# Two-layer network, second layer: delta-rule queues reordered, expert stage entered by batches

## Chip, core and metric

The kernel runs on one core of one Trainium2 chip, in a single program. The metric is the device time of one execution in microseconds (us). Before the change the median of three runs is 2874.5 us (2872.1 to 2878.21).

## What is computed

The reference is a network of two layers on x of shape (8, 512, 128): 8 batches of 512 tokens, all in float32. Layer 0 (attention with 16 heads, then 8 experts with top-1 routing) isn't touched. Layer 1, cut to what matters:

```
h = layernorm(x) * (1 + ca) + sa
q, k, v = split(silu(causal_conv(h @ W_qkv)))      # 16 value heads of 64, 8 key heads
per token t:  S = S * exp(g_t);  S = S + k_t (v_t - k_t S) * b_t;  o_t = q_t S
x = x + ga * ((rmsnorm(o) * norm_w * silu(h @ W_z)) @ W_out)
h = layernorm(x) * (1 + cb) + sb
scores = sigmoid(h @ gate_w.T)                     # 16 experts
each expert takes its 512 best tokens: silu(g) * up, down, times score, added back
shared = (silu(h @ sh_gate.T) * (h @ sh_up.T)) @ sh_down.T
x = x + gb * (experts + shared)
```

## The kernel before

The program is a row of stages. Each stage has its own semaphores and ends in a barrier of all engines (Stage.end), and in a stage every engine works off its own queue in the order in which it is written. Three stretches matter here.

**The delta rule** (delta1, main loop on lines 1896 to 2497). The 8 batches of 512 tokens are worked as 4 pairs of sequences beside each other: one chunk step k (0 to 31) takes 32 tokens of four batches at once, with two halves f of eight heads. An even and an odd step make a pair m = k // 2. The loop variable k runs from FIRST to LAST, and the work is staged: in the iteration of k, the projections and the causal convolution for k + 4 are made (project, conv, squash), the norms, the decayed products and the triangular solve for the pair m + 1 (norms, diag, attend, turn, initial, substitute, turn_back), the recurrence itself for k (read_out, residual, solve, weights, attend on TensorE, weigh, add_state, update, decay), and the output for k - 1 (square_out, squares, total, root_out, inverse_norm, gated, turned, output).

- VectorE has the long piece: substitute (lines 2106 and 2107), 30 rounds of two instructions for a pair, spread over the two steps. In an even step it also has norms, two attends (a scan on line 2082, two products on 2089 and 2092, a copy on 2093) and turn (2097). update (2122) subtracts what add_state (2424) put into a bank from the state S.
- GpSimd has window (1916), diag (1923), residual (1929), decay (1941), weigh (1950), gated (1957, 1961), initial (1979 to 1984). In an even step diag stands ahead of residual; diag waits for norms on VectorE.
- ScalarE has square_out (2184), roots (2190), root_out (2196), project (2204 to 2215), weights (2251), values (2239), squash (2226), keys (2257), gate (2245), turned (2263), output (2270).
- TensorE has project (2335), read_out (2374), norms (2324), similar (2395), solve (2407), values (2351), attend (2438), add_state (2424), keys (2359), gate (2344), turned (2447) and output (2454). Small products share two banks of PSUM in turn; the list MISC fixes their order, and TensorE and ScalarE count through it.

**The entry of the expert stage.** residual1 loads the delta rule's output for all 4096 tokens (Hr) and four modulation rows (MODB), and adds ga * Hr to X (2515, 2516). A second stage loads the router's and the shared expert's weights and turns them on TensorE (1179 to 1184), with copies on VectorE (1192 to 1196). A third, norm_router, makes the statistics of all 32 tiles (819, 822), then batch by batch scales on VectorE (829), modulates (833, 834), turns (884), routes (892), and computes the shared expert: hidden (901, 903), silu (871), product (817), down (912), output (860).

**The selection** (same function, the stage that begins on line 1215). The threshold of each expert is found by 30 steps of bisection (BITS):

```
for n in range(BITS):                       # VectorE, lines 1313 to 1320
    count scores >= cand per partition      # 1315
    nxt = cand | next bit                   # 1317
    wait for the sum over partitions        # TensorE, 1372
    cand = nxt ^ (bit if sum < 512)         # 1319, 1320
```

In the first 24 of these steps TensorE also turns one third of an expert's weights (1379, 24 such units for experts 0 to 7), which ScalarE copies to SBUF (1258), while SyncE loads further experts' weights into two buffers (fetch, 1209, 1210). After the loop VectorE computes ranks and one-hot masks (1322 to 1345), and TensorE the lists of slots (1399).

## Time and profile before

| | us |
|---|---|
| median of 3 runs | 2874.5 |
| the profiled execution: its own time | 2889.17 |
| the profiled execution: span | 2887.4 |
| TensorE busy | 2208.4 (76%) |
| VectorE busy | 1884.6 (65%) |
| ScalarE busy | 1313.1 (45%) |
| GpSimd busy | 847.9 (29%) |

The profile is of one execution. An engine's busy time is the union of its instructions' durations; waits are what lies between. In the views, PE is TensorE's matmul, PEld its weight load, DVE VectorE, ACT ScalarE, POOL GpSimd, SPq the queue of SyncE that issues DMAs. L2107 is line 2107 of the kernel. In a timeline, a row gives start, duration, engine, line, instruction, what it writes and reads, how many were merged (x4), and in brackets how long the engine was idle before it and for whom it waited. PEclk is the clock that TensorE was granted, as a share of 2.4 GHz.

### The profile page before, as it was taken

The numbers are of one execution on the slowest core, as the hardware profiler recorded it, in microseconds if no ns is written. First come the engines' busy times: TensorE is split into PE (matmuls) and PEld (weight loads), VectorE is DVE, ScalarE is ACT, GpSimd is POOL, SyncE is SP. The second block draws the span as 40 slices with busy tenths as digits, with TensorE's granted clock in tenths as the row PEclk, the third lists the DMA queues.
The fourth block names the chain that finished last, engine by engine and source line by source line (L and its number), as shares of the span: only waits on it lengthen the run. The fifth ranks groups of instructions, "written<-read, shape, count | busy, mean of one in ns | idle before, by whom it ended". The sixth has DMA issues, their size and how long they took to land. (4 is left out here: it accounts for less than half of the span.)

```text
span 2887.4 us, 63254 instructions
## 1 busy us (share of the span) xinstructions
PE 2208.4 (76%) x25656; PEld 1394.9 (48%) x25656; DVE 1884.6 (65%) x4425; ACT 1313.1 (45%) x2383; POOL 847.9 (29%) x877
## 2 busy tenths in 40 slices
PE   2798889888888573488888888888888862755984
PEld 0344444444444361355555555565555541544653
DVE  1477667767666226588888888888888834254433
ACT  0367667666655221555555555555555230121321
POOL 1000010100100240135555445444554530002885
PEclk8599889989978796579988888898988885757997
DMA  5000000000000412100000000000000002142334
GB/s 198 7 1 5 5 8 5 8 5 5 9 4 5 118 53 61 26 9 11 11 12 12 11 11 12 11 12 12 11 11 4 4 10 89 42 117 69 54 44 84
DMA packets 104290, 85.49 MB, mean 30 GB/s; under 512 B 22126, under 2 KB 90898, under 8 KB 103616
## 3 DMA queue, kind: packets, MB, share of 16 engines
q1 hardware_dynamic: 90432, 68.31, 8.0%
q0 software_dynamic: 13568, 13.14, 2.8%
q8 instruction: 203, 3.33, 0.5%
q14 instruction: 87, 0.71, 0.1%
HBM read 59.22 MB, written 22.71 MB: 28 GB/s over the span
## 5 line engine op out<-in xcount | busy, mean ns | idle before, releaser
L617 ACT ACTIVATE Pr<-Pr,nmax 128x512 f32<-128x512 f32 x512 | 341.2, 714 | 181.3 <-DVE nmax L552 179.0
L722 PE MATMUL bank<-ident,Pr 128*128 128x128 f32 x2048 | 322.6, 303 | 71.6 <-DVE PT L561 59.0
L722 PEld LDWEIGHTS bank<-ident,Pr 128*128 128x128 f32 x2048 | 249.2, 154 | 260.7 <-DVE PT L561 152.8
L552 DVE CUSTOM_DVE_ANT_0 Pr<-bank,Tb 128x512 f32<-128x512 f32 x512 | 331.1, 685 | 46.9 <-PE bank L708 46.9
L561 DVE COPY PT<-bank 128x512 f32<-128x512 f32 x256 | 176.5, 689 | 194.1 <-PE bank L736 189.1
L2351 PE MATMUL bank<-Wcv,hw 128*128 128x512 f32 x512 | 276.4, 690 | 7.5 <-POOL hw L1916 4.5
L2107 DVE TENSOR_TENSOR Tc<-Tc,pr 128x30 f32<-128x30 f32 (+14 forms) x480 | 209.1, 436 | 16.5
L624 ACT ACTIVATE PT<-bank 128x512 f32<-128x512 f32 x256 | 151.0, 590 | 121.4 <-PE bank L736 86.0
L2106 DVE TENSOR_TENSOR pr<-AC,Tc 128x30 f32<-128x30 f32 (+14 forms) x480 | 190.7, 397 | 17.5 <-POOL Tc L1984 3.7
L708 PE MATMUL bank<-kp,qp 8*128 8x512 f32 x1024 | 181.0, 707 | 1.1 <-DVE nmax L552 1.1
L2351 PEld LDWEIGHTS bank<-Wcv,hw 128*128 128x128 f32 x512 | 107.5, 221 | 131.5 <-issue 118.9
L2215 ACT ACTIVATE yp<-raw,cwq 128x256 f32<-128x256 f32 x384 | 160.1, 508 | 0.0
L736 PE MATMUL bank<-PT,vp 128*9 128x512 f32 x1024 | 156.1, 683 | 0.0
L432 POOL DMA_INDIRECT disp<-H,slot x32 | 31.8, 993 | 399.2 <-DVE slot L508 391.9
L2407 PE MATMUL bank<-Xs,Tt 32*32 32x64 f32 x4096 | 87.0, 243 | 67.4 <-POOL Xs L1929 67.4
L1929 POOL TENSOR_TENSOR Xs<-vt,Xs 128x512 f32<-128x512 f32 x64 | 94.6, 1488 | 149.2 <-DVE Xs L2019 149.2
L423 POOL TENSOR_SCALAR H<-X,rs,nm 128x128 f32<-128x128 f32 x32 | 14.0, 452 | 423.0 <-DVE nm L540 423.0
L2407 PEld LDWEIGHTS bank<-Xs,Tt 32*32 32x32 f32 x4096 | 76.8, 141 | 90.2 <-issue 68.1
L1941 POOL TENSOR_TENSOR S<-S,GC 128x1024 f32<-128x1024 f32 x60 | 114.6, 1909 | 0.0
L1438 POOL DMA_INDIRECT acc<-eo,ids x64 | 100.8, 1576 | 39.4 <-issue 18.6
L2374 PE MATMUL bank<-S,kq 64*32 64x128 f32 x4096 | 108.7, 275 | 2.4 <-DVE S L2122 2.4
L2122 DVE TENSOR_TENSOR S<-S,bank 128x512 f32<-128x512 f32 x120 | 76.9, 682 | 51.4 <-PE bank L2424 51.4
(397 smaller groups left out, 4419.1 us busy)
## 6 DMA issues: line engine op xcount, KB each, us to landing
aB<-alpha SPq DMA_DIRECT2D x64, 128.0 KB, 2.8
Tb<-scores SPq DMA_DIRECT2D x1, 7168.0 KB
w<-in_L_ffn_W SPq DMA_DIRECT2D x16, 256.0 KB, 5.8
rawW<-in_L_ffn_up_w SPq DMA_DIRECT2D x16, 256.0 KB, 3.0
rawW<-in_L_ffn_gw SPq DMA_DIRECT2D x16, 256.0 KB, 3.4
rawW<-in_L_ffn_down_w SPq DMA_DIRECT2D x16, 256.0 KB, 3.8
disp<-zero SPq DMA_DIRECT2D x1, 2580.0 KB, 15.6
xin<-disp SPq DMA_DIRECT2D x8, 322.5 KB, 6.4
```

The source lines that it names most:

```text
L552: V.tensor_tensor_reduce(out=Pr[:, s, i, :], in0=pS[hh][:, :], in1=Tb[:, h, at:at + L], scale=-1.0, scalar=3.0e38, op0=ALU.add, op1=ALU.mi ...
L561: V.tensor_copy(PT[:, m % NPS, :], pT[m % 2][:, :]).then_inc(r["b_evd"], 1)
L617: A_(Pr[:, s, i, :], Pr[:, s, i, :], ACT.Exp, scale=-1.0, bias=nmax[:, s, i:i + 1])\
L624: A_(PT[:, m % NPS, :], pT[m % 2][:, :], ACT.Copy).then_inc(r["b_eva"], 1)
L708: mm(pS[hh][:, :], qp[rows, G % SLOTS, i * P:(i + 1) * P], kp[rows, G % SLOTS, :], start=True, stop=True, tile_position=(32 * hh, 0)).then ...
L722: last = TR(pT[m % 2][:, t * P:(t + 1) * P], Pr[:, (G % 2) * HG + hh, t, j * P:(j + 1) * P], ident[:, :])
L736: mm(pO[32 * hh:32 * hh + HD0 + 1, :], vp[:, b % 2, j, G % NG * HG + hh, :], PT[:, m % NPS, :], start=(j == 0), stop=(j == LT - 1), tile_p ...
L2106: link(V.tensor_tensor(o, bcast(AC[:, i + 1:CK, i], 2, i), bcast(Tc[:, i, 0:i], 1, n), ALU.mult))
L2107: link(V.tensor_tensor(Tc[:, i + 1:CK, 0:i], Tc[:, i + 1:CK, 0:i], o, ALU.add))
L2215: last = A_(yp[:, i, j, :, :], raw[:, tp, j, :, i:i + 2 * CK], ACT.Copy, scale=tap(j, i))
L2351: last = mm(o[:, :], tokens(k, i), Wcv[:, i, 512 * f:512 * f + 512], start=(i == 0), stop=(i == KS - 1))
L2407: last = mm(BK[f][rows, DK * h:DK * h + DK], Tt[rows, :, k % 2, HF * f + h], Xs[rows, f, DK * h:DK * h + DK], start=True, stop=True, tile_ ...
```

## The change

Four things change.

1. Delta rule, output: the product with W_out for step k - 1 isn't issued at the end of the iteration of k any more, but in the next one, on TensorE behind the first projection and ahead of read_out, on ScalarE behind the first project. MISC has it in the new place, and the DMA out follows.
2. Delta rule, orders. GpSimd: both residuals ahead of diag, and initial ahead of the second decay. VectorE: both read_outs first, conv ahead of the second squares, the second conv between the two attends, inverse_norm behind turn (in an odd step behind the second conv), and rounds 18 to 30 of the substitution cut at 20 and 25. ScalarE: the second square_out behind project and output, weights(k, 0) ahead of the second project, root_out behind it.
3. Entry: the three stages become one (entry1), which goes batch by batch: load of Hr and of three rows, residual, statistics, root, scaling on GpSimd, modulation, turn, route. The shared expert is taken out of it; hT keeps the turned tokens of all 8 batches.
4. Selection: the shared expert is put between the counting steps. In steps 4b and 4b + 1 TensorE computes hidden(b, 0) and hidden(b, 1), in steps 4b + 2 and 4b + 3 the halves of down(b - 1), and every second step (12 in place of 24) turns a unit of weights; the other 12 units come behind the loop. VectorE has product in steps 4b + 1 and 4b + 2, ScalarE the silu and the copy out, SyncE the writes to acc between the loads of the experts 2 to 7.

The delta rule:

```diff
 
-            FIRST, LAST = -4, NS + 1
+            FIRST, LAST = -4, NS + 2
             MISC = []
             for k in range(FIRST, LAST):
                 if (k + 4) // 2 < NP:
                     MISC += [("pj", 2 * (k + 4))]
+                if 0 <= k - 2 < NS:
+                    MISC += [("out", k - 2)]
                 if k % 2 == 0 and 0 <= k // 2 + 1 < NP:
                     MISC += [("nm", k // 2 + 1)]
@@ -1864,7 +1935,7 @@
                 if 0 <= k < NS:
                     MISC += [("z", 2 * k), ("z", 2 * k + 1)]
                 if 0 <= k - 1 < NS:
-                    MISC += [("ot", 2 * (k - 1)), ("ot", 2 * (k - 1) + 1), ("out", k - 1)]
+                    MISC += [("ot", 2 * (k - 1)), ("ot", 2 * (k - 1) + 1)]
             USE = {key: u for u, key in enumerate(MISC)}
...
                         m, e = k // 2, k % 2
                         if 0 <= k + 1 < NS:
                             window(k + 1)
+                        if 0 <= k < NS:
+                            residual(k, 0)
+                            residual(k, 1)
                         if 0 <= m + 1 < NP and e == 0:
                             diag(2 * (m + 1))
                         if 0 <= k < NS:
-                            residual(k, 0)
-                            residual(k, 1)
                             decay(k, 0)
                         if 0 <= m + 1 < NP and e == 0:
                             diag(2 * (m + 1) + 1)
                         if 0 <= k < NS:
                             weigh(k, 0)
                             weigh(k, 1)
-                            decay(k, 1)
                         if 0 <= m + 1 < NP and e == 0:
                             initial(m + 1)
+                        if 0 <= k < NS:
+                            decay(k, 1)
                         if 0 <= k - 1 < NS:
...
                             squares(k - 1, 0)
                         if here:
                             read_out(k, 0)
+                            read_out(k, 1)
+                        if (k + 4) // 2 < NP:
+                            conv(2 * (k + 4))
                         if past:
                             squares(k - 1, 1)
                             total(k - 1)
-                        if here:
-                            read_out(k, 1)
-                        if (k + 4) // 2 < NP:
-                            conv(2 * (k + 4))
                         if ahead and e == 0:
                             norms(m + 1)
-                        if 0 <= k - 1 < NS:
-                            inverse_norm(k - 1)
-                        if ahead and e == 0:
                             attend(2 * (m + 1))
-                            attend(2 * (m + 1) + 1)
-                            turn(m + 1)
                         if ahead and e == 1:
                             substitute(m + 1, 12, 18)
                         if (k + 4) // 2 < NP:
                             conv(2 * (k + 4) + 1)
+                        if ahead and e == 0:
+                            attend(2 * (m + 1) + 1)
+                            turn(m + 1)
+                        if past:
+                            inverse_norm(k - 1)
+                        if ahead and e == 1:
+                            substitute(m + 1, 18, 20)
                         if here:
                             accumulate(k, 0)
                             update(k, 0)
                         if ahead and e == 0:
                             substitute(m + 1, 1, 6)
                         if ahead and e == 1:
-                            substitute(m + 1, 18, 24)
+                            substitute(m + 1, 20, 25)
                         if here:
                             accumulate(k, 1)
                             update(k, 1)
                         if ahead and e == 0:
                             substitute(m + 1, 6, 12)
                         if ahead and e == 1:
-                            substitute(m + 1, 24, CK - 1)
+                            substitute(m + 1, 25, CK - 1)
                             turn_back(m + 1)
 
                 @block.scalar
                 def _(act):
                     A_ = nc.scalar.activation
 
...
                         if past:
-                            square_out(k - 1)
+                            square_out(k - 1, 0)
                         if (k + 4) // 2 < NP:
                             project(2 * (k + 4))
+                        if 0 <= k - 2 < NS:
+                            output(k - 2)
+                        if past:
+                            square_out(k - 1, 1)
                         if k % 2 == 0 and 0 <= k // 2 + 1 < NP:
                             roots(k // 2 + 1)
+                        if here:
+                            weights(k, 0)
+                        if (k + 4) // 2 < NP:
+                            project(2 * (k + 4) + 1)
                         if past:
                             root_out(k - 1)
-                        if (k + 4) // 2 < NP:
-                            project(2 * (k + 4) + 1)
-                        if here:
-                            weights(k, 0)
                         if 0 <= k + 1 < NS:
                             values(k + 1, 0)
                         if here:
                         if past:
                             turned(k - 1, 0)
                             turned(k - 1, 1)
-                            output(k - 1)
...
                         if (k + 4) // 2 < NP:
                             project(2 * (k + 4))
+                        if 0 <= k - 2 < NS:
+                            output(k - 2)
                         if here:
                             read_out(k, 0)
                             read_out(k, 1)
...
                         if past:
                             turned(k - 1, 0)
                             turned(k - 1, 1)
-                            output(k - 1)
```

The entry (lines that only moved are left out):

```diff
+def entry1(nc, g, a, s, w, hT):
...
+        def _(sp):
+            def batch(b):
+                sp.dma_start(of(Hr, b), g["attn"][b * L:(b + 1) * L, :].rearrange("(t p) d -> p t d", p=P))\
+                  .then_inc(s[f"n_in{b}"], 16)
+                sp.dma_start(rows[:, b, :, :], bcast(g["mods"][1, b, GA:CB + 1, :], 0, P)).then_inc(s[f"n_in{b}"], 16)
+            batch(0)
...
+                sp.dma_start(d, v).then_inc(s["n_ld"], 16)
+            for b in range(1, B):
+                batch(b)
+            sp.dma_start(w["gbr"][:, :, :, :], mod_rows(g, 1, GB, GB + 1)).then_inc(s["n_db"], 16)
+            sp.dma_start(w["dbias"][:, :, :], bcast(a["L1_ffn_down_b"], 0, P)).then_inc(s["n_db"], 16)
...
+            def residual(b):
+                dve.wait_ge(s[f"n_in{b}"], 32)
+                link(V.tensor_tensor(of(Hr, b), of(Hr, b), row(b, GA), ALU.mult))
+                V.tensor_tensor(of(X, b), of(X, b), of(Hr, b), ALU.add).then_inc(s["n_x"], 1)
...
+            def inverse(b):
+                at = slice(b * LT, (b + 1) * LT)
+                dve.wait_ge(s["n_rstd"], b + 1)
+                link(V.reciprocal(rs[:, at], rs[:, at]))
+                V.scalar_tensor_tensor(nm[:, at], mv[:, at, 0], -1.0, rs[:, at], ALU.mult, ALU.mult)\
+                    .then_inc(s["n_nm"], 1)
+
+            def modulate(b):
+                dve.wait_ge(s["n_hs"], b + 1)
+                link(V.tensor_tensor(of(H, b), of(H, b), row(b, CB), ALU.mult))
+                V.tensor_tensor(of(H, b), of(H, b), row(b, SB), ALU.add).then_inc(s["n_h"], 1)
...
+            residual(0)
+            stats(0)
+            dve.wait_ge(s["n_t"], 1)
...
             for b in range(B):
+                if b + 1 < B:
+                    residual(b + 1)
+                inverse(b)
+                if b + 1 < B:
+                    stats(b + 1)
                 if b:
                     logits(b - 1)
-                    if shared:
-                        product(b - 1)
+                modulate(b)
...
+        @block.gpsimd
+        def _(pool):
+            for b in range(B):
+                pool.wait_ge(s["n_nm"], b + 1)
+                for n in range(b * LT, (b + 1) * LT):
+                    last = nc.gpsimd.tensor_scalar(H[:, n, :], X[:, n, :], rs[:, n:n + 1], nm[:, n:n + 1],
+                                                   ALU.mult, ALU.add)
+                last.then_inc(s["n_hs"], 1)
...
+            root(0)
             for b in range(B):
                 if b + 1 < B:
-                    turned(b + 1)
+                    root(b + 1)
+                act.wait_ge(s["n_xT"], b + 1)
+                A_(hT[:, b, :], PB[b % 2][:, :], ACT.Copy).then_inc(s["n_hT"], 1)
...
+            pe.wait_ge(s["n_e"], 1)
             for b in range(B):
-                if b + 1 < B:
-                    turn(b + 1)
+                turn(b)
                 route(b)
```

The selection, on VectorE and on TensorE (ScalarE follows TensorE's order):

```diff
+                    def product(b, c):
+                        dve.wait_ge(s["h_up"], 2 * b + c + 1)
+                        dve.wait_ge(s["h_sg"], 2 * b + c + 1)
+                        if b >= 2:
+                            dve.wait_ge(s["h_so"], b - 1)
+                        V.tensor_tensor(su[:, b % 2, c, :], PB[3 + c][:, :], sg[:, c, :], ALU.mult).then_inc(s["h_su"], 1)
...
                     for n in range(BITS):
                         bit = BITS - 1 - n
                         V.tensor_scalar(junk[:, :], sT[:, :], cand[:, :].bitcast(F32), None, ALU.is_ge, ALU.add,
                                         accum_out=acc[:, :]).then_inc(s["h_acc"], 1)
                         link(V.tensor_scalar(nxt[:, :], cand[:, :], (1 << bit) >> 1, None, ALU.bitwise_or))
+                        if n % 4 in (1, 2):
+                            product(n // 4, n % 4 - 1)
                         dve.wait_ge(s["h_cnt"], n + 1)
                         link(V.tensor_scalar(off[:, :], PB[1][:, 0:1], float(CAP1), float(1 << bit), ALU.is_lt, ALU.mult))
...
                     V.tensor_tensor_scan(cum[:, :], one[:, :], eq[:, :], 0.0, ALU.mult, ALU.add).then_inc(s["h_gt"], 1)
+                    product(B - 1, 1)
                     dve.wait_ge(s["h_nd"], 1)
...
+                    def prepare(m):
+                        e, kind = m // 3, m % 3
+                        pe.wait_ge(s[f"h_ld{e % 2}"], 48 * (e // 2 + 1))
+                        if m >= 3:
+                            pe.wait_ge(s["h_wte"], m - 2)
...
+                    def hidden(b, c):
+                        if b or c:
+                            pe.wait_ge(s["h_sg"], 2 * b + c)
+                        mm(PB[2][:, :], wg[:, c * P:(c + 1) * P], hT[:, b, :], start=True, stop=True)\
+                            .then_inc(s["h_gp"], 1)
+                        if b:
+                            pe.wait_ge(s["h_su"], 2 * (b - 1) + c + 1)
+                        mm(PB[3 + c][:, :], wu[:, c * P:(c + 1) * P], hT[:, b, :], start=True, stop=True)\
+                            .then_inc(s["h_up"], 1)
+
+                    def down(b, t0):
+                        pe.wait_ge(s["h_su"], 2 * b + 2)
+                        if b:
+                            pe.wait_ge(s["h_soe"], b)
+                        for t in (t0, t0 + 1):
+                            for c in range(2):
+                                last = mm(PB[0][:, t * D:(t + 1) * D], su[:, b % 2, c, t * P:(t + 1) * P],
+                                          wd[:, c, :], start=(c == 0), stop=(c == 1))
+                        if t0:
+                            last.then_inc(s["h_so"], 1)
                     pe.wait_ge(s["h_mk"], 1)
                     for n in range(BITS):
                         pe.wait_ge(s["h_acc"], n + 1)
                         mm(PB[1][:, 0:1], blk[:, :], acc[:, :], start=True, stop=True).then_inc(s["h_cnt"], 1)
-                        if n < 3 * EA:
-                            e, kind = n // 3, n % 3
-                            pe.wait_ge(s[f"h_ld{e % 2}"], 48 * (e // 2 + 1))
-                            if n >= 3:
-                                pe.wait_ge(s["h_wte"], n - 2)
-                            for c in range(FC):
-                                last = TR(PB[5 + kind][:, c * P:(c + 1) * P], raw[:, e % 2, kind, c, :], ident[:, :])
-                            last.then_inc(s["h_wt"], 1)
+                        b, u = n // 4, n % 4
+                        if u < 2:
+                            hidden(b, u)
+                        elif b:
+                            down(b - 1, 2 * (u - 2))
+                        if early(n) is not None:
+                            prepare(early(n))
+                    prepare(LATE)
...
+                    down(B - 2, 0)
+                    down(B - 2, 2)
                     pe.wait_ge(s["h_sel"], 1)
                     mm(PB[1][:, 2:3], low[:, :], cum[:, L - 1:L], start=True, stop=True).then_inc(s["h_pre"], 1)
+                    prepare(LATE + 2)
+                    prepare(LATE + 3)
+                    down(B - 1, 0)
+                    down(B - 1, 2)
                     pe.wait_ge(s["h_pos"], 1)
```

gbr holds the rows for the last residual; the old stages and residual1 are removed.

## Rows read from the trace of the kernel before

**Rows 1.** Windows of the run: span, busy time of each engine, granted clock, DMA.

```profile
core 0: us, PE busy (x) PEld busy (x) DVE busy (x) ACT busy (x) POOL busy (x), PEclk, DMA share, GB/s
...
1218.80:2269.20 1050.40, 884.77 (x16777) 616.13 (x16775) 903.81 (x1752) 559.67 (x1154) 507.18 (x529) 0.88 0.04 11
...
2380.20:2417.40 37.20, 2.54 (x9) 1.54 (x9) 10.23 (x8) 0.00 (x0) 0.00 (x0) 0.50 0.47 154
2417.40:2529.40 112.00, 74.54 (x288) 53.01 (x288) 41.24 (x138) 19.86 (x34) 0.00 (x0) 0.75 0.13 38
...
2533.20:2580.60 47.40, 37.59 (x146) 27.91 (x146) 28.44 (x126) 14.33 (x24) 0.00 (x0) 0.50 0.50 140
```

**Rows 2.** The tile AC: count, min/median/max ns, first and last start.

```profile
L2097 DVE STREAM_TRANSPOSE AC<-A x16: 1245/1245/1247, 1218.8 to 2269.2; 128x1024 f32<-128x1024 f32 x16
L1979 POOL TENSOR_TENSOR AC<-AC,rkT x16: 1909/1913/1918, 1220.2 to 2272.1; 128x1024 f32<-128x1024 f32 x16
L1981 POOL TENSOR_SCALAR_AFFINE_SELECT Tc<-AC x16: 1266/1267/1267, 1222.1 to 2274.1; 128x1024 f32<-128x1024 f32 x16
```

**Rows 3.** Waits of VectorE from 1218.8 to 2269.2 us (total, times, longest).

```profile
DVE S L2122 <- PE bank L2424: 43.6, 27, 3.6
DVE bank L2070 <- ACT yp L2215: 25.9, 27, 1.0
DVE Lt L2082 <- POOL Lt L1923: 18.4, 16, 1.2
DVE A L2089 <- PE bank L2395: 13.5, 15, 2.1
DVE pr L2106 <- POOL Tc L1984: 3.5, 11, 1.5
```

**Rows 4.** Timeline of TensorE, an odd step (1716.5 to 1749.3 us).

```profile
1727.45 1.09 PE L2438 MATMUL bank<-Ws,Pt 32*32 32x64 f32 x64 [2.12 <-ACT Ws L2251]
1728.48 5.40 PE L2351 MATMUL bank<-Wcv,hw 128*128 128x512 f32 x8
```

**Rows 5.** Timeline of TensorE in the router stage: hidden, down, hidden.

```profile
2434.40 2.05 PE L901 MATMUL bank<-hT,wg 128*128 128x512 f32 x2
...
2517.36 2.05 PE L912 MATMUL bank<-wd,su 128*128 128x128 f32 x16
2519.24 1.02 PE L901 MATMUL bank<-hT,wg 128*128 128x512 f32 x2
```

**Rows 6.** Timeline of GpSimd and TensorE, the even step behind rows 4.

```profile
1757.30 1.05 POOL L1923 TENSOR_TENSOR Lt<-bk,d 128x512 f32<-128x512 f32 x1 [15.82 <-DVE rkd L2061]
...
1759.72 1.94 PE L2407 MATMUL bank<-Xs,Tt 32*32 32x64 f32 x64 [4.19 <-POOL Xs L1929]
```

**Rows 7.** Timeline of the entry on VectorE: residual, statistics, modulation.

```profile
2394.76 4.42 DVE L2515 TENSOR_TENSOR Hr<-Hr,MODB 128x4096 f32<-128x4096 f32 x1 [29.38 <-DMA Hr<-attn]
...
2417.38 6.29 DVE L819 BATCH_NORM_STATS2 st<-X 128x6 f32<-128x128 f32 x32 [0.93 <-PEq L86]
...
2427.97 0.69 DVE L833 TENSOR_TENSOR H<-H,MODB 128x512 f32<-128x512 f32 x1
```

**Rows 8.** Timeline of VectorE: the substitution's smallest shape, behind initial and at the end.

```profile
1703.72 0.98 DVE L2106 TENSOR_TENSOR pr<-AC,Tc 128x30 f32<-128x30 f32 x1 [0.19 <-POOL Tc L1984]
...
1747.70 0.19 DVE L2106 TENSOR_TENSOR pr<-AC,Tc 128x30 f32<-128x30 f32 x1
```

**Rows 9.** The scaling of the tile H on GpSimd in layer 0 (L423).

```profile
L423 POOL TENSOR_SCALAR H<-X,rs,nm x32: 445/452/454, 260.0 to 959.1; 128x128 f32<-128x128 f32 x32
```

**Rows 10.** Timeline of TensorE in the bisection: a count and a unit of turning.

```profile
2535.96 0.58 PE L1372 MATMUL bank<-hits,blk 128*128 128x1 f32 x2 [0.35 <-DVE junk L1315]
2536.41 1.09 PE L1379 MATMUL bank<-ident,rawW 128*128 128x128 f32 x4
```

**Rows 11.** Groups of VectorE, 1218.8 to 2269.2 us: the substitution.

```profile
L2107 DVE TENSOR_TENSOR Tc<-Tc,pr 128x30 f32<-128x30 f32 (+14 forms) x450 | 193.4, 430 | 15.5
L2106 DVE TENSOR_TENSOR pr<-AC,Tc 128x30 f32<-128x30 f32 (+14 forms) x450 | 176.6, 392 | 16.4 <-POOL Tc L1984 3.5
```

331 lines of the change are left out of this document (143 added, 188 removed).

## The prediction

> **What bounds the kernel now.** I cut the run into windows first, at the places where the code changes stage, since a busy share over the whole run mixes stages with different limits. The change touches four of them [rows 1]: the steady part of the delta rule, 1050.4 us; the residual and the loads ahead of the router, 37.2; the router with the shared expert, 112.0; and the bisection, 47.4 for 25 of its 30 steps. Look at three things in these rows. In the delta rule VectorE is busy 903.8 of 1050.4 us (86%) and TensorE 884.8 (84%): either may bound it, and both wait. In the 37.2 us almost nothing computes. In the router stage TensorE is busy 74.5 of 112 us at a mean clock of 0.75, VectorE 41.2: nothing is full, the engines take turns. In the bisection the clock is 0.50 throughout, though TensorE is busy for 37.6 of 47.4 us.
>
> The delta rule's period comes from a tile written once for each pair of steps: 16 times from 1218.8 to 2269.2 us, so 1050.4 / 15 = 70.0 us a pair [rows 2]. The waits of VectorE in this window sum to 106.6 us with a sixth one of 1.7 [rows 3], that is 7.1 us a pair. VectorE's queue is nearly gapless otherwise, so a pair can't get shorter than about 70.0 - 7.1 = 62.9 us however the other engines are ordered.
>
> **Delta rule, wait by wait.** The instructions stay the same, so what counts is which of these waits goes and what is late next.
> - *S on add_state, 43.6 us.* In odd steps attend on TensorE waited 2.12 us for Ws, since weights stands behind ScalarE's second project, and the eight matmul instructions after it took 5.40 us [rows 4]; two of this width take 2.05 us at half clock and 1.02 at full clock [rows 5], so that this was partly a half-clock stretch behind an idle one. In even steps solve waited 4.19 us for the residual on GpSimd, which stood behind diag, and diag had waited 15.82 us for VectorE's norms [rows 6]. Residual ahead of diag and weights ahead of the second project remove both. What is late next: in even steps TensorE meets the second similar, which may only overwrite its bank when the first attend on VectorE is through, some 2 us after TensorE gets there. Kept: 1 us a pair, 15 us.
> - *The bank on yp, 25.9.* The first conv waits for project, which stood behind two square_outs, the second of them held by VectorE's squares. Now only one stands ahead. Kept: 0. The second project now waits for solve in its place, through weights; conv for it comes behind the whole first attend, which covers that.
> - *The scan on Lt, 18.4.* The second attend waited; three conv instructions now stand between. But the first diag (1.05 us) [rows 6] runs between norms and the first scan, and inverse_norm, which filled that, is moved behind turn. Kept: 0.75 a pair, 11 us.
> - *A on similar, 13.5.* Same cover. Kept: 0.
> - *The substitution on Tc, 3.5.* Behind turn GpSimd has initial, 1.91 + 1.27 us and a small memset [rows 2]. Conv, accumulate and update covered that; now it is inverse_norm, accumulate and update only, about 2.4 us. This wait grows to 0.8 a pair, 12 us.
>
> Kept in all 15 + 11 + 12 = 38 us, gained 106.6 - 38 = 68 us, or 4.5 a pair. Bounds: 107 if none is left; at the other end nothing, or less (rivals). Output a place later: TensorE runs the first project while ScalarE copies OT, so it no longer stalls ahead of output; that is in the sum already, as read_out comes earlier. The DMA out has a whole step to land, and SyncE's gates pass it only in order: nothing. The extra iteration holds one output that ended the loop before too: nothing.
>
> **Entry.** Before: 37.2 + 112.0 = 149.2 us [rows 1]. After: the first batch's Hr and rows are loaded first, then weights, turns and copies. The weight stage took 13.8 us: from 2394.76 + 2 x 4.42 = 2403.6 to 2417.4 [rows 1, 7]. Its largest load (1 MB) now comes last, batch 0 comes first instead; I keep 13.8, and residual(0) and stats(0) lie inside it. Then eight rounds on VectorE. One round: residual 2 x 0.69 [rows 7]; inverse, two tiny ones, 0.4 (the 30-element op alone takes 0.19 [rows 8]); then the scaling on GpSimd, 4 x 0.452 = 1.81 [rows 9], beside which VectorE makes the next statistics (6.29 / 8 = 0.79 and less for the aggregates [rows 7]) and the logits; then modulation 2 x 0.69. With 0.3 for hand-overs: 1.38 + 0.4 + 1.81 + 1.38 + 0.3 = 5.3, times 8 = 42. TensorE's turn and route of the batch before lie beside it. The tail is turn (four transposes, like a unit of the bisection), a copy, route (half the products of a down, 2.05 at most), the last write and the barrier (0.93 us of idling ahead of the statistics): I estimate 6. Sum 13.8 + 42 + 6 = 62. The loads (some 5.7 MB against 4 MB in the 14.6 us before the first instruction there) run ahead of rounds of 5.3 us. Gain 149 - 62 = 87 us; between 78 (rounds of 6.4) and 94.
>
> **Bisection.** The old step is 47.4 / 25 = 1.9 us. TensorE had 1.09 us of turning in it and still 0.35 us idle before the next count [rows 10], so about 1.45 us a step are free. At full clock hidden needs four such instructions, 2 x 1.02 less their overlap, 1.7 us, half a down 2.05 / 2 = 1.0 [rows 5], a unit of turning 0.55. Over four steps the excess is 0.3, 0.8 (hidden and unit), 0, 0.1: 1.2, times 7.5 = 9 us. VectorE's product (0.69) lies where VectorE waits for the count: 2 us in all. Behind the loop 1. At half clock hidden is 3.5, half a down 1.9, a unit 1.09: excess 2.0, 3.1, 0.5, 1.6 = 7.2, times 7.5 = 54 us, 57 with the rest. So it is 12 at one end, 57 at the other. The nearest row is the router stage's clock of 0.75, with idle stretches that the new loop lacks; the bisection's 0.50 is of turning and counting alone [rows 1]. I take 16. The last 8 units of turning lie beside the 48 instructions in which VectorE makes the masks: nothing.
>
> **Sum.** -68 - 87 + 16 = -139 us, on the profiled execution's 2889.17: 2750. It stands 0.5% above the median of 2874.5, and I carry the difference over: 2735 as a median.
>
> **Rivals.**
> 1. *The bisection stays at half clock.* For: 0.50 over 47 us at 79% busy. Against: that work was turning, and in the router stage the same products reached full clock, 1.02 for 2.05 [rows 5]. Then -68 - 87 + 57 = -98: 2776. Chance 0.14.
> 2. *The delta rule gains little.* The second similar waits, TensorE's clock halves behind it, and values and add_state come later by as much as the removed idle time gave. For: rows 4 show such a stretch behind 2.12 us. Then I give it 20 us instead of 68: -91: 2783. Chance 0.17.
> 3. *VectorE becomes the floor.* No wait is left, rounds of the entry are 4.5 us: -107 - 93 + 10 = -190: 2685. Chance 0.13.
> 4. *Slower: VectorE is held up by GpSimd in more places.* The substitution takes (193.4 + 176.6) / 15 = 24.7 us a pair [rows 11]; its smallest shape takes 0.19 us in one place and 0.98 where GpSimd's gated runs [rows 8]. Its place now: decay(k, 1) and gated both come behind initial, on top of substitute(1, 6). By what these rows show one meeting costs 0.8 us. For the whole kernel to be slower by over 0.2% it must cost (139 + 6) / 16 = 9 us a pair, eleven more meetings in each; at 10 us a pair the time would be 2735 + 160 = 2895. For: GpSimd has 529 / 15 = 35 instructions a pair [rows 1], so there are enough of them. Against: their number stays, and the old order has such meetings too. Up to 4.5 us a pair it only eats the delta rule's gain. Chance 0.03.
>
> The Trainium skill, page "SBUF — State Buffer", section "SBUF: two separate sides", has the rule for rival 4: a VectorE instruction with two inputs in SBUF and a GpSimd instruction that reads SBUF exclude each other for the whole instruction, with no sharing. The trace agrees (0.98 us against 0.19 for one shape), and by that rule an order alone can make VectorE's instructions longer or shorter.
>
> That the change doesn't do what it says, I give nothing: each move is written out in the queues.
>
> **Numbers.** The forecast has 0.53. Its own range is 2700 to 2765 (entry +-9, delta +-25, bisection -6 to +20). With the rivals: 2675 to 2790. About 0.2%, 6 us, is what a measurement can tell from no change. Faster: 0.53 + 0.14 + 0.17 + 0.13 = 0.97, less 0.01 that falls within 0.2%: 0.96; slower 0.03.
>
> **What the profile after would show.** The tile AC at intervals of 65.5 us; VectorE's wait on add_state below 20 us, on yp near 0, on Tc up to about 12; solve and attend no longer waiting over 2 us. From the end of the delta rule to the bisection 62 us. Count to count 1.9 to 2.5 us, with a clock near 1 there. I am wrong on the delta rule if the interval stays above 68 us, or if the substitution's sum grows by more than 3 us a pair; on the entry if the GpSimd scaling takes over 2.5 us a batch; on the bisection if the clock stays at 0.50.

## The result and the profile after

The changed kernel takes 2805.03 us (median of 4 runs, 2798.69 to 2808.58), the kernel before 2876.36 us in 4 runs beside it: a ratio of 0.9743 with a 95% interval of 0.9708 to 0.9778. It is faster, by 71 us, about half of the 139 us forecast, and outside the range of 2675 to 2790.

The windows of the run after, cut at the same stage boundaries, the columns those of [rows 1]:

```profile
0.00:1142.00 1142.00, 867.46 (x5183) 469.57 (x5184) 691.37 (x2012) 586.08 (x944) 114.10 (x155) 0.86 0.10 32
...
1197.50:2271.80 1074.30, 914.75 (x16775) 646.04 (x16774) 939.89 (x1745) 554.64 (x1151) 489.03 (x529) 0.85 0.04 11
...
2379.90:2440.80 60.90, 27.64 (x109) 22.20 (x109) 37.41 (x137) 8.96 (x20) 15.03 (x37) 0.50 0.47 140
2440.80:2501.80 61.00, 55.43 (x267) 36.39 (x268) 43.03 (x166) 20.41 (x34) 0.00 (x0) 0.95 0.36 97
```

and the tile AC, which answers to [rows 2]:

```profile
L2170 DVE STREAM_TRANSPOSE AC<-A x16: 1245/1245/1246, 1197.5 to 2271.8; 128x1024 f32<-128x1024 f32 x16
```

The profiled execution took 2798.69 us, 90.5 less than the one of before. By stage:

| stage | before, us | after, us | difference |
|---|---|---|---|
| up to the first AC (layer 0 and the delta rule's start) | 1218.8 | 1197.5 | -21.3 |
| AC to AC, 15 intervals | 1050.4 | 1074.3 | +23.9 |
| last AC to the entry | 111.0 | 108.1 | -2.9 |
| entry, from the end of the delta rule to the first count | 153.0 | 60.9 | -92.1 |
| bisection, 30 steps | 57.2 | 61.0 | +3.8 |
| the rest of the span | 297.0 | 294.9 | -2.1 |

Three things are to be read here. The entry did what was said of it. The bisection cost a quarter of what was said, at a granted clock of 0.95. And the delta rule, which was to gain 68 us, lost 24: the interval is 1074.3 / 15 = 71.6 us, where 70.0 was and 65.5 was forecast. The first line is not the change's: in e1_entry_only below, whose code up to there is that of before, the first AC comes at 1198.6 us, and in the other runs anywhere from 1188.4 to 1213.7.

Where VectorE and TensorE wait in that window (total, times, longest), to be held against [rows 3]:

```profile
DVE bank L2143 <- ACT yp L2288: 39.8, 13, 3.2
DVE rkq L2125 <- ACT rkq L2263: 21.1, 13, 4.0
DVE Lt L2155 <- POOL Lt L1994: 15.8, 16, 1.2
DVE S L2195 <- PE bank L2500: 5.5, 5, 3.1
...
PE bank L2500 <- DVE S L2195: 82.7, 27, 5.8
```

The waits on S (43.6 us, now 5.5) and A (now 0.2) are gone, as forecast. But yp, which was to wait for nothing, takes 39.8 us, rkq, for which it had waited 1.7 us in all, 21.1, and all of them, four small ones included, come to 93.1 us. The last line is the mirror image: TensorE, which waited 12.8 us for VectorE's state update before, now waits 82.7 for it. VectorE's busy time also rose, from 903.8 [rows 1] to 939.9 us. Its groups with the largest change (busy us, mean ns), in the window of after:

```profile
L2179 DVE TENSOR_TENSOR pr<-AC,Tc 128x30 f32<-128x30 f32 (+14 forms) x450 | 201.3, 447 | 16.0 <-POOL Tc L2055 3.6
L2180 DVE TENSOR_TENSOR Tc<-Tc,pr 128x30 f32<-128x30 f32 (+14 forms) x450 | 192.9, 429 | 15.5
...
L2119 DVE TENSOR_TENSOR nrm<-nrm,rkq 128x16 f32<-128x16 f32 x27 | 37.6, 1392 | 0.9
...
L2112 DVE TENSOR_TENSOR rq<-rkq 128x8 f32<-128x8 f32 x28 | 15.2, 542 | 1.0
...
L2166 DVE COPY dl<-Lt 128x16 f32<-128x16 f32 x30 | 6.4, 214 | 0.0
```

The same instructions took 370 us (the first two, [rows 11]), 13.8, 4.7 and 24.1 us before, at means of 492, 166 and 777 ns for the last three.

### The profile page after: what moved, and what is told of

The parts are those of the page before. It is cut to its first block and busy times, and to the rows that moved or that the text cites. A ratio compares the mean times of both kernels' runs of the same rounds, so it can differ in the third digit from the quotient of the medians.

```text
span 2796.7 us, 63261 instructions
## 1 busy us (share of the span) xinstructions
PE 2193.0 (78%) x25656; PEld 1397.8 (50%) x25656; DVE 1922.3 (69%) x4429; ACT 1308.5 (47%) x2389; POOL 842.6 (30%) x909
## 5 line engine op out<-in xcount | busy, mean ns | idle before, releaser
L722 PEld LDWEIGHTS bank<-ident,Pr 128*128 128x128 f32 x2048 | 238.5, 149 | 254.4 <-DVE PT L561 154.0
L722 PE MATMUL bank<-ident,Pr 128*128 128x128 f32 x2048 | 310.9, 294 | 69.5 <-DVE PT L561 59.2
L2427 PE MATMUL bank<-Wcv,hw 128*128 128x512 f32 x512 | 263.3, 661 | 8.5 <-POOL hw L1987 5.2
L2179 DVE TENSOR_TENSOR pr<-AC,Tc 128x30 f32<-128x30 f32 (+14 forms) x480 | 215.9, 450 | 16.9 <-POOL Tc L2055 3.6
L2500 PE MATMUL bank<-Ud,Kt 32*64 32x128 f32 x1920 | 79.4, 311 | 93.4 <-DVE S L2195 87.7
L736 PE MATMUL bank<-PT,vp 128*9 128x512 f32 x1024 | 150.4, 659 | 0.0
L2000 POOL TENSOR_TENSOR Xs<-vt,Xs 128x512 f32<-128x512 f32 x64 | 80.8, 1275 | 209.1 <-DVE Xs L2092 209.1
L423 POOL TENSOR_SCALAR H<-X,rs,nm 128x128 f32<-128x128 f32 x32 | 13.9, 448 | 404.9 <-DVE nm L540 404.9
L2500 PEld LDWEIGHTS bank<-Ud,Kt 32*64 32x64 f32 x1920 | 63.4, 153 | 120.9 <-issue 105.3
L2411 PE MATMUL bank<-hTa,Wqk 128*128 128x256 f32 x256 | 97.3, 519 | 17.9 <-ACT bank L2282 8.9
L2021 POOL TENSOR_TENSOR Ud<-Ws,dl 128x512 f32<-128x512 f32 x60 | 63.4, 1056 | 147.8 <-ACT Ws L2324 147.8
```

Of the source, the lines that this page charges most:

```text
L722: last = TR(pT[m % 2][:, t * P:(t + 1) * P], Pr[:, (G % 2) * HG + hh, t, j * P:(j + 1) * P], ident[:, :])
L736: mm(pO[32 * hh:32 * hh + HD0 + 1, :], vp[:, b % 2, j, G % NG * HG + hh, :], PT[:, m % NPS, :], start=(j == 0), stop=(j == LT - 1), tile_p ...
L2179: link(V.tensor_tensor(o, bcast(AC[:, i + 1:CK, i], 2, i), bcast(Tc[:, i, 0:i], 1, n), ALU.mult))
L2427: last = mm(o[:, :], tokens(k, i), Wcv[:, i, 512 * f:512 * f + 512], start=(i == 0), stop=(i == KS - 1))
L2500: last = mm(BK[x % 2][64 * r:64 * r + 64, P * q:P * q + P], Kt[rows, k % 2, P * q + 64 * r:P * q + 64 * r + 64], Ud[rows, r, P * q:P * q + ...
```

## The experiments

Each run was made beside the kernel before on the same chip, and the ratios are to that. "Interval" is AC to AC, first to last over 15, in one profiled execution of each kernel. It came out as 70.03 and 70.01 us in the two kernels that have the delta rule of before, and as 71.62 and 71.61 in the two that have the changed one, so I read differences of 0.3 us and more from it. The last column is the time for which add_state on TensorE waited for the state update S; waits of read_out for S aren't in it (15.0 us in f3, 18.1 in i1, 16.4 in i2, at most 5.9 in the others).

| run | median, us | ratio, 95% interval | interval, us | VectorE busy, us | TensorE on S, us |
|---|---|---|---|---|---|
| before | 2876.36 | | 70.03 | 903.8 | 12.8 |
| after | 2805.03 | 0.9743 [0.9708, 0.9778] | 71.62 | 939.9 | 82.7 |
| e1_entry_only | 2786.29 | 0.9685 [0.9641, 0.9729] | 70.01 | 904.4 | 12.8 |
| e2_delta_only | 2899.29 | 1.0096 [1.0066, 1.0126] | 71.61 | 940.2 | 84.7 |
| e3_weights_back | 2798.3, one run | | 70.71 | 930.9 | 62.2 |
| e4_inverse_back | 2821.1, one run | | 72.31 | 931.3 | 79.4 |
| f1_pool_only | 2773.55 | 0.9655 [0.9615, 0.9695] | 68.79 | 914.6 | 15.0 |
| f2_vector_only | 2838.84 | 0.9891 [0.9837, 0.9944] | 73.70 | 933.8 | 39.9 |
| f3_output_only | 2818.25 | 0.9821 [0.978, 0.9862] | 72.37 | 915.6 | 12.8 |
| f4_scalar_only | 2947.12 | 1.025 [1.0211, 1.0289] | 80.55 | 918.0 | 131.9 |
| g1_output_in_place | 2811.6 | 0.9781 [0.9737, 0.9824] | 72.53 | 945.9 | 83.4 |
| g2_pool_back | 2806.1 | 0.9765 [0.9719, 0.981] | 71.20 | 932.0 | 84.8 |
| g3_cut_20_25 | 2840.26 | 0.9895 [0.9853, 0.9937] | 73.95 | 938.8 | 71.5 |
| g4_cut_and_rows_ahead | 2796.92 | 0.9728 [0.9678, 0.9779] | 70.95 | 927.1 | 13.1 |
| h1_cut_back | 2739.14 | 0.9536 [0.9506, 0.9566] | 67.31 | 936.8 | 28.5 |
| h2_vector_no_cut | 2794.32 | 0.9742 [0.9704, 0.978] | 71.23 | 917.1 | 14.8 |
| h3_one_row | 2802.47 | 0.9761 [0.9729, 0.9793] | 71.55 | 923.7 | 42.0 |
| h4_residual_only | 2759.38 | 0.9593 [0.9558, 0.9629] | 68.51 | 913.2 | 24.5 |
| i1_inverse_sooner | 2731.46 | 0.951 [0.9459, 0.956] | 66.97 | 905.8 | 17.6 |
| i2_and_initial_back | 2730.93 | 0.9525 [0.9472, 0.9579] | 66.39 | 907.3 | 17.7 |

### The change in two halves

e1_entry_only is the changed kernel with the function delta1 of before; e2_delta_only is the kernel before with delta1 of after.

> The delta rule's function is that of before; entry and selection are the changed ones. Theory: the whole gain lies in entry and selection (94 us less in the entry, 4 us more in the bisection) and the delta rule's reordering gave back some 24 us. Then this kernel takes 2876 - 88 = 2788 us, less than the changed kernel's 2805, and the tile AC comes at intervals of 70.0 us. Rival (the traces' difference in the delta rule is a matter of the execution, not of the orders): the interval is 71.6 here as well and the time that of the changed kernel, 2805.

> The kernel before with the changed kernel's delta rule alone. Theory: AC at intervals of 71.6 us, 15 to 16 of them, so 2876 + 20 = 2896 us, 0.7% slower than before. Rival: no difference (interval 70.0, 2876 us).

The entry and the bisection alone beat the whole change, 0.9685 against 0.9743 (the 95% intervals of the two overlap by a little, their runs, up to 2791.14 us and from 2798.69 us on, don't), and the delta rule alone is slower than nothing, 1.0096. Both came as expected. Each has the interval and the waits of the kernel whose delta1 it has, so the two halves don't touch one another.

### Two moves undone

e3_weights_back puts weights back behind the second project on ScalarE; e4_inverse_back puts inverse_norm back behind norms on VectorE, with ScalarE's root_out where that needs it.

```
 ScalarE, e3:                      VectorE, e4:
-  weights(k, 0)                    norms(m + 1)
+  root_out(k - 1)                 +inverse_norm(k - 1)
   project(2 * (k + 4) + 1)         attend(2 * (m + 1))
-  root_out(k - 1)                  ...
+  weights(k, 0)                   -inverse_norm(k - 1)
```

> The changed kernel, on ScalarE alone root_out and the second project stand ahead of weights(k, 0) again. Theory: VectorE's second conv waited 39.8 us for yp because project stood behind weights, and weights behind solve; with the old order this wait is below 5 us, the wait on add_state returns only in odd steps, by under 20 us; the interval of AC falls by 1 to 2 us to about 70. Rival (VectorE's lengthened instructions are the whole cause): the wait moves but the interval stays within 0.5 us of 71.6.

> The changed kernel; inverse_norm stands behind norms again, ahead of the first attend, and on ScalarE root_out ahead of weights and of the second project, so that inverse_norm needn't wait for them. Theory: the product nrm by rkq, 1.39 us on average now because GpSimd's initial runs at the same time, falls to 0.5 us or less, 24 us in the stretch; the first scan's wait for GpSimd (15.8 us) falls below 8; the interval falls by 1.5 to 2.5 us. Rival: the length moves to other instructions (accumulate, substitution, the copy dl, 0.78 before and 0.21 now) and the interval stays within 0.5 us of 71.6.

With weights back yp's wait is 0, but a wait of 24.1 us on A and one of 19.3 on S stand in its place, and the interval falls by 0.9 us only. With the inverse back its own group falls to 13.7 us as expected, but the substitution grows to 414.9 us and S costs 31.7: the interval rises where a fall was expected. Both missed on the interval: the name on the longest wait was not its cause, since taking it away only renamed it.

### The four orders, one at a time

On e1_entry_only, each run takes one queue's hunk of the change's diff: GpSimd's (f1), VectorE's (f2), the output product a place later on all engines (f3), ScalarE's (f4). f1 and the core of f3:

```
 GpSimd, f1:                          f3 (MISC; ScalarE, TensorE, SyncE alike):
+  residual(k, 0), residual(k, 1)        MISC += [("pj", 2 * (k + 4))]
   diag(2 * (m + 1))                  +  if 0 <= k - 2 < NS:
-  residual(k, 0), residual(k, 1)     +      MISC += [("out", k - 2)]
   ...                                   ...
-  decay(k, 1)                        -  ..., ("out", k - 1)]
   initial(m + 1)
+  decay(k, 1)
```

> The new entry and bisection with the delta rule of before, whose one change is GpSimd's order: both residuals ahead of diag, initial ahead of decay(k, 1). In the rest of the delta rule all is as before. Without it the interval from AC to AC is 70.0 us and the time about 2786 us. Theory A (the loss of the changed kernel is VectorE's own order, by which it comes to yp and rkq before they are there): the interval stays within 0.4 us of 70.0 and the time at 2780 to 2792. Theory B (the loss is in the collisions with GpSimd, whose longest work now falls on VectorE's long rows): the interval grows by 0.8 us or more, the time to 2800 or more, and nrm<-nrm,rkq L2119 or the substitution takes longer than in before (492 ns and 370 us in all).

> The new entry and bisection with the delta rule of before, whose one change is VectorE's order: both read_outs and the first conv ahead of the second squares, one attend, the second conv, the other attend, inverse_norm late, the substitution cut at 20 and 25. Theory A: the loss is here: interval 71.0 or more, time 2800 or more, with waits on yp and rkq of 20 us and more each, since VectorE asks for them sooner and ScalarE still gives them late. Theory B (collisions that come from GpSimd's order): within 0.4 us of 70.0. Theory C (ScalarE's order makes yp late): the yp wait is under 10 us and the interval under 70.5.

> The new entry and bisection with the delta rule of before, whose one change is that the output product and all that belongs to it (PE, ScalarE's copy, SyncE's DMA) come a place later, behind the next first project. Theories A, B and C all say that this part does no harm by itself: TensorE doesn't wait for VectorE's turned output as long, and add_state's 12.8 us of waits on PE fall or stay. Interval 69.3 to 70.2, time 2775 to 2790. If it is instead this part that costs (the copy of the output now stands ahead of the second square and roots on ScalarE, 0.5 us or so a place), the interval is 71 or more.

> The new entry and bisection with the delta rule of before, whose one change is ScalarE's order: the first project ahead of the second square, weights(k, 0) ahead of the second project, root_out behind it; the output stays in its place. Theory C (the loss is that weights wait for PE's solve and hold up the second project): interval 71 or more with a wait on yp of 20 us or more. Theory A: VectorE takes the second conv late here, behind both attends, so yp is there: wait on yp under 5 us, and A's or S's wait falls since weights come earlier; but root_out now stands behind the second project, and inverse_norm is early in VectorE's order of before, so a wait on it shows up, some 10 to 20 us in all; interval 69.5 to 70.7.

GpSimd's order is a gain by itself (-1.2 us an interval), the first clear one; theory B falls. VectorE's costs 3.7, with yp at 42.9 us, so theory A stood for the moment. The output product costs 2.4 by itself. None of the three theories said so; the expectation named such a cost only as the other case, and put it down to ScalarE's copy. The rows point elsewhere: output took a turn between the first project and the norms, and the two banks for such products are given out in turn, so that the norms (L2396) and the second project (L2407) now need the bank that the first project just filled, and wait for ScalarE to copy it. Waits of TensorE in f3_output_only:

```profile
PE bank L2396 <- ACT bank L2280: 54.8, 13, 4.5
PE bank L2407 <- ACT bank L2280: 41.0, 13, 3.5
```

ScalarE's order alone costs 10.5 us an interval, far from either theory. Its root_out comes late while VectorE's inverse_norm is still early, 28 waits of 6.7 us. Waits of VectorE in f4_scalar_only:

```profile
DVE nrm L2114 <- ACT nrm L2264: 187.9, 28, 8.9
```

The single effects sum to +15.4 us, the four together to +1.6: two orders that are made for each other can't be priced apart.

### Taking parts out of the whole, and one small piece alone

g1 and g2 are the changed kernel with the output in its old place, and with GpSimd's old order. g3 and g4 go from f1 (GpSimd's new order, the best so far) and add one small piece of VectorE's order, the cut of the substitution: rows 18 and 19 ahead of the state update in the odd places.

```
 VectorE, g3 against f1:                 g4 besides:
-  substitute(m + 1, 12, 18)             +  substitute(m + 1, 12, 14)
+  substitute(m + 1, 12, 20)                conv(2 * (k + 4))
   conv(2 * (k + 4) + 1)                    ...
   accumulate(k, 0)                      -  substitute(m + 1, 12, 20)
   update(k, 0)                          +  substitute(m + 1, 14, 20)
-  substitute(m + 1, 18, 24)                conv(2 * (k + 4) + 1)
+  substitute(m + 1, 20, 25)
   ...
-  substitute(m + 1, 24, CK - 1)
+  substitute(m + 1, 25, CK - 1)
```

(conv stands behind the rows in both, as in the kernel before.)

> The changed kernel whose output product, its copy and its DMA stay at the end of their own place (the other three orders are the changed ones). Theory D, from the output product alone (72.37 us in place of 70.01): with the output between the first project and the norms, TensorE's norms need the bank that the first project has just filled, and wait until ScalarE has copied it, so rkq comes late. Without it the wait of VectorE on rkq falls from 21.1 us to under 5, and the interval of the changed kernel, 71.62, falls by 1 to 2 us, to 69.6 to 70.6; time 2775 to 2792. The rival: in the changed orders the norms are late for another reason (the project itself is asked for late), and the output's place has no effect: rkq still 15 to 25 us, interval 71.3 to 71.9, time about 2805.

> The changed kernel with GpSimd's order of before (diag ahead of the residuals, decay(k, 1) ahead of initial). GpSimd's order alone, on the old orders, gave 1.2 us an interval. If its gain is its own (the copy of dl no longer meets GpSimd, 24.0 to 5.5 us, and A's wait falls from 15.5 to 3.7), the interval of the changed kernel grows from 71.62 to 72.4 to 73.2, time 2817 to 2830. The rival: its gain hangs on the other orders, and with the changed ones its collisions (nrm<-nrm,rkq 37.6, rq 15.2 us) are its price: then the interval stays at 71.3 to 71.9 or falls, and L2119 and L2112 fall back to 14 and 5 us.

> The new entry and bisection, GpSimd's new order, and of the rest of the delta rule's change only the cut of the substitution: rows 18 and 19 ahead of accumulate and update in the odd places, not behind (12 to 20, 20 to 25, 25 to 31). In the kernel with GpSimd's order alone VectorE waits 2.3 us for add_state in every odd place, right behind accumulate; the two rows take 1.75 us. If they fill that wait, S's 25.3 us of waits fall by 15 or more and the interval from 68.79 to 67.3 to 68.1, time 2752 to 2766. The rival: the wait is only moved, since the second update and the products behind it start 1.75 us later in TensorE's and ScalarE's orders, or the two rows meet GpSimd: interval 68.6 to 69.2, time 2770 to 2780.

> As the cut at 20 and 25 on GpSimd's new order, and with rows 12 and 13 of the substitution ahead of the first conv in the odd places, where VectorE waits 0.95 us for yp. If the row work fills that wait too, yp's 22.0 us fall to about 10 and the interval lies 0.6 to 1.0 under that of the cut alone, 66.5 to 67.5, time 2740 to 2758. The rival: conv comes 0.8 us later, so squash, and the squares behind it on ScalarE, come later and the wait turns up at rkq or at the next yp: interval no lower than with the cut alone.

None came out as its theory said. Without the late output the changed kernel is slower, 72.53 for 71.62, though it costs 2.4 alone: with the other orders new it gains 0.9. Without GpSimd's order it is no slower (71.20), as g2's rival had it, but the two groups that were to fall back to 14 and 5 us (L2119 and L2112 above) are at 29.7 and 15.3. And the two rows that should have filled a wait of 2.3 us cost 5.2 us an interval. g4 has the same cut, and beside it two other rows taken from behind the first conv of the odd place to ahead of it: its interval is 70.95 us, 3.0 less than g3's, and add_state's wait for S falls from 71.5 us to 13.1. So rows ahead of the update don't all cost alike. With six rows between the first conv and the update again, as in f1, most of the loss is gone; which of g4's two differences from f1 makes the 2.2 us that remain, no run shows. The cut is the largest effect of so small a piece, and it is in the changed kernel too. The changed kernel's odd place, on VectorE from the second conv to the second update:

```profile
1721.54 1.22 DVE L2119 TENSOR_TENSOR nrm<-nrm,rkq 128x16 f32<-128x16 f32 x1
1722.68 0.39 DVE L2179 TENSOR_TENSOR pr<-AC,Tc 128x234 f32<-128x234 f32 x1
1723.11 1.13 DVE L2180 TENSOR_TENSOR Tc<-Tc,pr 128x234 f32<-128x234 f32 x1
1724.27 1.36 DVE L2179 TENSOR_TENSOR pr<-AC,Tc 128x228 f32<-128x228 f32 x1
1725.66 1.12 DVE L2180 TENSOR_TENSOR Tc<-Tc,pr 128x228 f32<-128x228 f32 x1
1726.82 0.69 DVE L2201 TENSOR_TENSOR O<-O,bank 128x512 f32<-128x512 f32 x1
1727.42 1.28 DVE L2195 TENSOR_TENSOR S<-S,bank 128x512 f32<-128x512 f32 x2
```

on GpSimd:

```profile
1720.83 1.90 POOL L2012 TENSOR_TENSOR S<-S,GC 128x1024 f32<-128x1024 f32 x1
1722.84 1.13 POOL L2028 TENSOR_TENSOR O<-O,nrm 128x512 f32<-128x512 f32 x1
1724.12 1.26 POOL L2032 TENSOR_TENSOR O<-O,zs 128x512 f32<-128x512 f32 x1
1725.34 1.19 POOL L2028 TENSOR_TENSOR O<-O,nrm 128x512 f32<-128x512 f32 x1
1726.67 1.27 POOL L2032 TENSOR_TENSOR O<-O,zs 128x512 f32<-128x512 f32 x1
```

and on TensorE:

```profile
1722.68 1.09 PE L2514 MATMUL bank<-Ws,Pt 32*32 32x64 f32 x64
1728.85 1.98 PE L2500 MATMUL bank<-Ud,Kt 32*64 32x128 f32 x32 [5.07 <-DVE S L2195]
1730.76 1.11 PE L2435 MATMUL bank<-ident,kq 128*128 128x128 f32 x4
...
1742.00 5.02 PE L2400 MATMUL bank<-bd,sqc 128*128 128x2 f32 x32
```

A row takes 0.4 + 0.4 us undisturbed. Beside GpSimd's gated output three of the four instructions end some 0.25 us after one of GpSimd's and take 1.1 to 1.4 us: 4.1 us from 1722.68 to the accumulate, where 1.75 was expected. Behind them stands the update, behind that TensorE's second add_state, which idles 5.07 us. Behind the idle time TensorE runs slower as well: this add_state takes 1.98 us, where the first one of the same place (1721.64) took 1.10, and the norms take 5.02, where they take 4.44 in h1 below. Over the window an instruction of add_state takes 312 ns on average, 273 before and 278 in h1, and the granted clock of the window, 0.88 before, is 0.85.

### The cut

h1 is the changed kernel with the old cut, everything else new:

```
-                        if ahead and e == 1:
-                            substitute(m + 1, 18, 20)
                         if here:
                             accumulate(k, 0)
                             update(k, 0)
...
-                            substitute(m + 1, 20, 25)
+                            substitute(m + 1, 18, 24)
...
-                            substitute(m + 1, 25, CK - 1)
+                            substitute(m + 1, 24, CK - 1)
```

h2 is f1 with VectorE's new order but the old cut. h3 is f1 with one row (18) ahead of the update instead of two. h4 is f1 with initial behind decay(k, 1) again, so that only the residuals' move is left.

```
 VectorE, h3 against f1:              GpSimd, h4 against f1:
-  substitute(m + 1, 12, 18)          +  decay(k, 1)
+  substitute(m + 1, 12, 19)             initial(m + 1)
   ...                                -  decay(k, 1)
-  substitute(m + 1, 18, 24)
+  substitute(m + 1, 19, 24)
```

> The changed kernel with the substitution cut as before: rows 18 and 19 behind accumulate and update of the odd places again, all else as changed. Theory E, from the cut alone on GpSimd's new order (68.79 to 73.95 us an interval): in their new place the two rows run while GpSimd works through Ud, decay and the gated output, each instruction takes 1.1 to 2.0 us in place of 0.40, update comes some 4 us later, TensorE's second add_state idles 5 us for it, and behind that idle time its granted clock is halved through keys, gates, norms and the first solve. With the cut back TensorE's wait for S falls from 82.7 us to under 35, the wait on rkq (21.1) to under 8, the interval from 71.62 to 68.5 to 70.3, and the time to 2758 to 2785. The rival: in the changed kernel VectorE is late at the update for its whole order (yp 39.8 us of waits, nrm<-nrm,rkq 37.6 us), the cut only shares it; then TensorE's wait stays over 55 us and the interval is 71.0 or more.

> GpSimd's new order and VectorE's new order without its cut of the substitution, on the new entry and bisection; ScalarE and the output as before. VectorE's whole new order cost 3.7 us an interval when alone. Theory E: the cut was nearly all of it, so this kernel is within 0.8 us of the one with GpSimd's order alone: interval 68.3 to 69.6, time 2766 to 2785. The rival: conv ahead of the second squares makes the waits for yp (42.9 us in the run with VectorE's order alone), and this stays: interval 70.3 or more, time 2795 or more, with yp over 35 us.

> GpSimd's new order alone, with one row of the substitution (18) ahead of accumulate and update in the odd places; two rows cost 5.2 us an interval. Theory E (a row is stretched by GpSimd to some 2.3 us or more, the update's own wait of 2.3 us takes it up once, and only what is over it makes TensorE idle and halves its clock): one row mostly fills the wait, the longest wait of TensorE for S is 1 to 3.5 us, interval 69.0 to 71.0, far less than half of the 5.2. The rival: each row ahead of the update costs its length in proportion: interval 71.2 to 71.6.

> On the new entry and bisection, of GpSimd's new order the residuals ahead of diag alone; initial stays behind decay(k, 1). GpSimd's whole order gave 1.22 us an interval (70.01 to 68.79). If the residuals are its cause (the solve gets Xs sooner: TensorE's 60.9 us of waits for Xs fell to 5.0), the interval is 68.3 to 69.2 and the substitution is back at 371 us from 390, since initial no longer runs beside its first rows at another time. The rival: initial ahead of decay is what takes GpSimd away from the copy of dl (24.0 to 5.5 us): then dl is back at 20 us or more and the interval at 69.5 to 70.2.

h1 brings the changed kernel to 2739 us, 67.3 us an interval, under the 68.5 to 70.3 that was expected. The cut alone is worth 4.3 us an interval, 65 us. Its window and waits:

```profile
1201.10:2210.80 1009.70, 892.96 (x16775) 625.14 (x16774) 936.79 (x1746) 555.60 (x1151) 492.76 (x530) 0.88 0.04 11
```

```profile
DVE Lt L2155 <- POOL Lt L1994: 15.9, 16, 1.2
DVE bank L2143 <- ACT yp L2286: 6.6, 6, 3.2
DVE S L2195 <- PE bank L2498: 5.2, 6, 2.0
DVE pr L2179 <- POOL Tc L2055: 3.6, 1, 3.6
DVE rkq L2125 <- ACT rkq L2261: 1.1, 1, 1.1
...
PE bank L2498 <- DVE S L2195: 28.5, 27, 1.6
```

VectorE is as busy as with the new cut, 936.8 for 939.9 us. The two rows are stretched in their old place too, as the same place of h1 shows:

```profile
1700.58 1.27 DVE L2195 TENSOR_TENSOR S<-S,bank 128x512 f32<-128x512 f32 x2
1701.77 1.08 DVE L2179 TENSOR_TENSOR pr<-AC,Tc 128x234 f32<-128x234 f32 x1
1702.88 1.12 DVE L2180 TENSOR_TENSOR Tc<-Tc,pr 128x234 f32<-128x234 f32 x1
1704.04 1.37 DVE L2179 TENSOR_TENSOR pr<-AC,Tc 128x228 f32<-128x228 f32 x1
```

There nobody waits for them. So what the rows cost depends on what stands behind them: TensorE's wait on S falls by 54.2 us, its busy time by 21.8 (914.8 to 893.0, at a clock of 0.88 again), and VectorE's waits from 93.1 to 32.4 us, yp and rkq with them. Those two had been echoes of TensorE's lateness. The 4.3 us are about the 4.1 by which the rows put off the accumulate and the update in the place shown; undisturbed, by their 0.4 us an instruction, they would have put them off by 1.7. The cut also takes row 24 from behind the second update to ahead of it. No run has that part alone; h3 lacks it, and shows the cost without it.

h2 was a miss: with the old cut VectorE's order on ScalarE's old one still gives 71.2, with yp at 47.4 us. h1 has ScalarE's new order and the late output besides, with yp at 6.6 us; no run tells the two apart there. h3 refutes the threshold that I expected: one row costs 2.8 us an interval, two cost 5.2. The wait of 2.3 us for S that it should have filled still shows 18.7 us in 14 times. Each row at this place costs nearly in proportion. h4 came as expected and shows that the residuals are all of the gain in GpSimd's order: 68.51 with them alone, 68.79 with initial moved too; the 0.3 between these two is at the limit of what can be told.

### What is left of the stretch

```
 VectorE, i1 against h1:
+  inverse_norm(k - 1)        (e == 1)
   conv(2 * (k + 4) + 1)
+  inverse_norm(k - 1)        (e == 0)
   attend(2 * (m + 1) + 1)
   turn(m + 1)
-  inverse_norm(k - 1)
```

i2 is i1 with initial behind decay(k, 1) again.

> The changed kernel with the cut of the substitution as before, and inverse_norm moved to where GpSimd should be idle: ahead of the second conv in the odd places, right behind it (ahead of the second attend) in the even ones. In the kernel with the cut back, nrm<-nrm,rkq takes 37.4 us (1386 ns each, 0.17 where it meets nothing) and always stands beside a GpSimd operation on two SBUF operands. Theory F (the stretch is a collision, and VectorE, 937 us busy of 1010, now sets the interval): L2119 falls to 5 to 15 us, and the interval by 1.3 to 2.3 us, from 67.31 to 65.0 to 66.0; time 2705 to 2722. The rival: GpSimd's gated output starts sooner and meets the substitution instead, which grows by as much; or the inverse waits for ScalarE's root: interval 66.8 to 67.6, time 2732 to 2745.

> As with inverse_norm sooner, and on GpSimd initial behind decay(k, 1) again. On the kernel with GpSimd's order alone this half of the order was worth nothing or a small loss (68.79 with it, 68.51 without, the substitution 390 and 375 us, the copy of dl 5.5 and 20.1). If that holds here, the interval is 0.1 to 0.6 under that of the kernel with inverse_norm sooner alone. The rival: VectorE now comes to the first rows sooner and waits for Tc (3.6 us once in the other), since initial ends 1.9 us later: a wait of 1.5 us or more in each pair, and an interval 0.5 to 1.5 higher.

The group of i1, to be held against 37.4 us and 1386 ns in h1, and its window and largest wait:

```profile
L2119 DVE TENSOR_TENSOR nrm<-nrm,rkq 128x16 f32<-128x16 f32 x28 | 5.7, 203 | 1.0
```

```profile
1207.90:2212.40 1004.50, 875.56 (x16779) 612.87 (x16779) 905.83 (x1747) 554.86 (x1151) 494.07 (x530) 0.90 0.04 11
```

```profile
DVE S L2195 <- PE bank L2500: 32.4, 15, 4.8
```

The collision is gone as expected: -31.7 us in the group, -31.0 in VectorE's busy time, and the substitution did not take it over (395.5 for 394.9 us). But the window is only 5.2 us shorter, since VectorE now waits 32.4 us for S: at 66.97 us the interval lies in the rival's range, though neither of the rival's causes shows. It looks as if VectorE and the chain through TensorE were about equally long in h1 and i1, so that shortening one alone gives little; no run shortens the chain through TensorE alone to show it. In its trace i2 is another 0.6 us an interval shorter, at the edge of what was expected, with other waits: the one on Tc grew from 4.1 to 19.3 us and the one on S fell from 32.4 to 10.9. The times don't bear this gain out: both kernels have a median of about 2731 us, each with runs from about 2717 to 2747, and the trace of i1 is of one of its longer runs (2740.59) and that of i2 of one of its shorter (2719.94). Their ratios can't be told from that of h1.

## Why the prediction was right and wrong

- **Delta rule, "The instructions stay the same, so what counts is which of these waits goes and what is late next."** This sentence is where it failed, twice. First, the moves were priced for each wait on the list, and the one move that no wait on the list named, rows 18 and 19 ahead of the state update, had no price at all. It costs 4.3 us an interval in the changed kernel, shown by h1. The rows have a position before the one operation for which TensorE waits, and that should have been asked of every moved row: who waits behind it. Second, the instructions stayed but their durations did not. VectorE's busy time grew by 36 us, 2.4 us an interval, mostly in operations that stand beside GpSimd's, the meetings that rival 4 described: the substitution +24.2 us, L2119 +23.8, L2112 +10.5, the copy of dl -17.7. The stretch also made the cut as dear as it is, 4.1 us for the two rows where 1.7 would be their own.
- **The waits kept, 38 us.** With the cut out of the way (h1) they are 32.4 us: S 5.2 against 15 expected, yp 6.6 against 0, Lt 15.9 against 11, A 0 against 0, Tc 3.6 against 12. The sum held by luck, with errors of 5 to 10 us in the terms that cancel. From 65.5 the interval h1 differs by (936.8 - 903.8) / 15 = 2.2 us of busy time less (38 - 32.4) / 15 = 0.4 of waits: 67.3, which is what it measured. So of the 6.1 us that the forecast missed, 4.3 are the cut and 1.8 the stretch. In the changed kernel the 38 are 93.1, with yp at 39.8 where nothing was kept, and rkq, for which nothing was kept either, at 21.1.
- **The output a place later** was taken as harmless. By itself it is not, for the two banks' turns (f3); among the other new orders it gains 0.9 us (g1 against after).
- **Entry, -87 us:** -92.1. The 60.9 us of the table hold 3.8 between the stage's end and the first count, which the forecast's 62 leaves out, so that 57 stand against 62. The rounds of 5.3 us were as worked out; one starts 5.33 us behind the other:

```profile
2398.61 0.68 DVE L862 TENSOR_TENSOR H<-H,MODB 128x512 f32<-128x512 f32 x1
...
2403.94 0.68 DVE L862 TENSOR_TENSOR H<-H,MODB 128x512 f32<-128x512 f32 x1
```

- **Bisection, +16 us:** +3.8, under its range of 12 to 57. The clock is 0.95, as at the full-clock end; the excess is what was too large. It was put at 1.2 us over four steps, with hidden sticking out by 0.3 and hidden with a unit of turning by 0.8. In the steady part the counts below are 2.04, 2.38, 1.62 and 1.68 us apart, 7.72 in all, where four old steps took 7.6: the two steps with a hidden are longer by 0.1 and 0.5, and the two without are shorter by 0.3 and 0.2, as their count takes 0.38 us where it took 0.58 at half clock [rows 10]. The working had let no step become shorter. Most of the 3.8 us is in the first two steps, 7.2 us, whose first products still take 2.05 us, at half clock.

```profile
2452.17 0.38 PE L1430 MATMUL bank<-hits,blk 128*128 128x1 f32 x2 [0.81 <-DVE junk L1340]
...
2454.21 0.28 PE L1430 MATMUL bank<-hits,blk 128*128 128x1 f32 x2
...
2456.59 0.28 PE L1430 MATMUL bank<-hits,blk 128*128 128x1 f32 x2
...
2458.21 0.38 PE L1430 MATMUL bank<-hits,blk 128*128 128x1 f32 x2 [0.34 <-DVE junk L1340]
...
2459.89 0.38 PE L1430 MATMUL bank<-hits,blk 128*128 128x1 f32 x2
```

- **Rivals.** Rival 1 is out (clock 0.95). Rival 2 was nearest in its sense, that TensorE falls behind an idle time and gives the gain back, but it looked for the place in the even step at the second similar; it was in the odd step at the second add_state, and cost more than all of the gain. It allowed 20 us of gain and got 24 of loss. Rival 3 is out. Rival 4 was right on the mechanism: VectorE's busy time grew by 2.4 us an interval, under its 4.5. It looked for all of it in the substitution, which grew by 1.6; as much again is in one operation of 16 elements (L2119, +1.6).
- Of the signs named ahead one told it: an interval above 68 us was to mean that the delta rule's term is wrong, and it is 71.6. The other, a substitution longer by over 3 us a pair, stayed silent at 1.6.

The forecast of 2735 us is within 0.2% of h1, the changed kernel without the cut. That is luck, and no credit to the working, which missed a line of the diff. Against the profiled execution of before, h1's 15 intervals gain 40.7 us where 68 was said, and everything behind the last AC gains 94.0 where 71 was said (87 less 16): the two errors nearly cancel.

## What to carry over

When a queue's order is rewritten, list every moved piece, not every wait, and ask of each what stands behind it on its own engine and which engine waits for that; two rows of 1.7 us that were to fill a gap of 2.3 us ahead of a handover cost 5.2 us an interval (g3), and beside their neighbours they took 5.9 us in the odd place of its trace (1739.85 to 1745.70). A wait that a profile names may be an echo: before it is chased, look at whether the engine it names had itself been held up, and by whom. Price paired moves on two engines together, and test the whole less one piece as well as one piece alone: the output's place costs 2.4 us an interval alone and gains 0.9 beside the other new orders.

## What the runs showed of the hardware

Whether a VectorE instruction is stretched beside GpSimd depends on its operands more than on its length. In the place shown, nrm<-nrm,rkq, 16 elements from two SBUF tiles, takes 1.22 us and a row's instructions 1.1 to 1.4, while O<-O,bank and S<-S,bank, which have one operand in PSUM, keep their 0.68 us (means of 679 and 683 ns after, 682 in e1_entry_only), though GpSimd works beside them as well: the accumulate at 1726.82 takes 0.69 beside GpSimd's O<-O,zs, which runs from 1726.67 to 1727.94. The reciprocal just ahead of L2119 keeps its 226 ns too. The Trainium skill, page "SBUF — State Buffer", section "SBUF: two separate sides", has it so: VectorE is locked out for a whole GpSimd instruction if it reads two SBUF operands or works in a two-port mode. The copy of dl, with one SBUF operand, has a mean of 1110 ns in g2_pool_back and 184 ns in f1_pool_only; by the page that would be the two-port mode, and no run here shows which it is.

The second point is how little of such a stretch matters. 31 us of it taken away gave 5 us in the trace (i1), while the same two stretched rows cost 65 us more in one place than in the other (after against h1).
